# The order of VectorE's two maxima and its copy in each half of an attention quad

## The chip, the core and the metric

The kernel runs on one core of a Trainium2 chip. The time is the device time of one execution in microseconds, the median of several runs. TensorE (PE) does the matrix products and the transposes, VectorE (DVE) and ScalarE (ACT) read their results out of eight PSUM banks, GpSimd (POOL) does part of the elementwise work, SyncE (SP) issues DMAs. Each engine runs its own list of instructions strictly in the order in which the program writes them, and waits for the other engines through counters.

## What is computed

Four layers one after another on x of shape 4 x 512 x 512 in float32: a sparse-mask attention with grouped heads (layer 0), full attention with one key head and a gated MLP (layer 1), cosine attention and an MLP (layer 2), and a mixture of small per-chunk MLPs (layer 3). All are conditioned by a vector per batch. The change touches the softmax of the first three:

```python
# layer 0: 16 heads of 32, 4 key heads; keys limited by a block mask
scores = jnp.einsum('bhtd,bhsd->bhts', q, k_exp) / jnp.sqrt(jnp.asarray(HEAD_DIM, x.dtype))
scores = jnp.where(mask[None, None], jnp.asarray(-jnp.inf, x.dtype), scores)
attn = jax.nn.softmax(scores, axis=-1)
y = jnp.einsum('bhts,bhsd->bhtd', attn, v_exp)
# layer 1: 8 heads of 64, one key head, no mask
attn = jax.nn.softmax(scores, axis=-1)
# layer 2: 16 heads of 32
scores = jnp.einsum('bhqd,bhkd->bhqk', qn, kn) + attn_bias
p = jax.nn.softmax(scores, axis=-1)
```

## The kernel before

Attention is cut into units: one head and one tile of 128 queries. Layers 0 and 2 have 64 units per batch (16 heads x 4 query tiles), layer 1 has 32, and with 4 batches that makes 256, 128 and 256 units. In layer 0 a unit has 1 to 4 key tiles of 128, since later blocks are masked; in layers 1 and 2 always 4. Four neighbouring units form a quad, so the layers have 64, 32 and 64 quads.

A unit goes through these steps (class `Heads`):

- scores (PE, L655): q times k into one of four PSUM banks, the bank being the unit's number modulo 4 (banks 0 to 3).
- max (DVE): in layers 0 and 2 one instruction reads the scores' bank and the bias, writes their negated sum to the probability buffer `Pr` and leaves the row maximum in `nmax` (L735, with a short second record that reads the accumulator); it frees the scores' bank. In layer 1 a plain reduction (L739); there the exponential reads the bank and frees it.
- exp (ACT, L765): reads `Pr` (layer 1: the bank), writes `Pr`, sums the row.
- turn (PE, L663): transposes of `Pr`, one for each key tile, into bank 4 or 5 in turns.
- copy: the turned tile goes from PSUM to `PT`, on ACT for the quad's even units (L770), on DVE for the odd ones (L742).
- values (PE, L679): `PT` with v into bank 6, once for every 4 or 8 units; then out (ACT, L777), recip (DVE, L747), spread (PE, L689) and divide (DVE, L753) per block of 128 channels.

The function `weave` writes the one order from which all four engines take their lists. Its loop goes over quads. In round t it writes the scores of the four units of quad t+1, then the first half: turns 0 and 1 of quad t, the ACT copy of unit 0, max and exp of unit 0 of quad t+1, the DVE copy of unit 1, max and exp of unit 1 of quad t+1. Then come a point for other work, spreads, values of quad t-1, another point, and the second half with units 2 and 3 in the same pattern, and two more points. At the points `weave` inserts "side" work of other batches and layers: norms (L261 to L352), projections (L388), the rotary step (L426 to L451), output projections (L1281), for layer 2 also the query and key norms (L479 to L522), the splitting of MLP weights (L1064, L1068). After each attention stretch comes an MLP (L1024), after the last the experts of layer 3.

Which waits an instruction carries is worked out by the program: `claim` makes a PE step wait for the step that last read its bank, so the scores of unit n wait for the max (layer 1: the exp) of unit n-4, a turn waits for the copy of the turn two before. A wait that an earlier wait of the same engine already covers is left out.

Below, turn i, copy i, max i and exp i mean unit i of a quad, 0 to 3. In round t turns and copies belong to quad t, maxima and exponentials to quad t+1, and the scores that open round t+1 belong to quad t+2.

Of the kernel before, what the change touches and what calls it, by code (L numbers as in the profile page):

```python
# [832 lines left out]
def weave(tab, mains, sides, opening=(), closing=()):  # L833

    seq, quads = [], []
    for m, (h, b) in enumerate(mains):
        h.first[b] = len(tab.units)  # L840
        tab.units += [(h, b, u) for u in range(h.U)]
        for g in range(h.U // h.G):
            tab.group_number[(h.name, b, g)] = len(tab.groups)
            tab.groups.append((h, b, g))
        quads += [(m, h, b, q) for q in range(h.U // 4)]

    per = [sum(q[0] == m for q in quads) for m in range(len(mains))]
    at_point = {(0, i): list(ops) for i, ops in enumerate(opening)}
    at_point.update({(len(mains), i): list(ops) for i, ops in enumerate(closing)})
    for m, count in enumerate(per):  # L850
        points = 4 * count
        for i, ops in enumerate(sides[m]):
            at_point.setdefault((m, (2 * i + 1) * points // (2 * len(sides[m]))), []).extend(ops)
    seen = [0] * (len(mains) + 1)

    def point(m):
        seq.extend(at_point.get((m, seen[m]), []))
        seen[m] += 1

    def units(t):  # L860
        if 0 <= t < len(quads):
            _, h, b, q = quads[t]
            return [(h, b, 4 * q + i) for i in range(4)]
        return []

    def turn(t, i):
        for h, b, u in units(t)[i:i + 1]:
            seq.append((h, b, "pe", "turn", u))

    def copy(t, i):  # L870
        for h, b, u in units(t)[i:i + 1]:
            seq.append((h, b, "dve" if i % 2 else "act", "copy", u))

    def soft(t, i):
        for h, b, u in units(t)[i:i + 1]:
            seq.extend([(h, b, "dve", "max", u), (h, b, "act", "exp", u)])

    spreads = []
    for t in range(-1, len(quads) + 2):
        m = quads[t + 1][0] if t + 1 < len(quads) else len(mains)  # L880
        for h, b, u in units(t + 1):
            seq.append((h, b, "pe", "scores", u))
        turn(t, 0)
        turn(t, 1)
        copy(t, 0)
        soft(t + 1, 0)
        copy(t, 1)
        soft(t + 1, 1)
        point(m)
        for h, b, c in spreads:  # L890
            seq.extend([(h, b, "pe", "spread", c), (h, b, "dve", "divide", c)])
        spreads = []
        for h, b, u in units(t - 1)[3:]:
            if (u + 1) % h.G == 0:
                g = h.group(u)
                seq.append((h, b, "pe", "values", g))
                if g % 2:
                    seq.extend([(h, b, "act", "out", g // 2), (h, b, "dve", "recip", g // 2)])
                    spreads.append((h, b, g // 2))
        point(m)  # L900
        turn(t, 2)
        turn(t, 3)
        copy(t, 2)
        soft(t + 1, 2)
        copy(t, 3)
        soft(t + 1, 3)
        point(m)
        point(m)
    assert not spreads and seen[len(mains)] >= len(closing)
    return seq  # L910
# [194 lines left out]
def conditioned_stack(nc, a, out):  # L1105
    ctx = ExitStack()
    with ctx:
# [409 lines left out]
        def ahead(stage):  # L1517
# [11 lines left out]
        sides01.append(beats((norm1b, 0)) + [[]] * 4 + among(beats((post1, 2)), beats((pair1, 0)) + mlp1.split(0)) +  # L1529
                       beats((norm1b, 1), (pair1, 1), (norm1b, 2)) + [[]])  # L1530
        attention01 = weave(tab, [(heads0, b) for b in range(B)] + [(heads1, b) for b in range(B)], sides01,
                            closing=[[], first[0], [], first[1], first[2], first[3]])
        qk = beats((qk2, 0))
# [7 lines left out]
        sides2.append(beats((norm2b, 0)) + among(beats((post2, 2)), beats((pair2, 0)) + mlp2.split(0)) +  # L1541
                      beats((norm2b, 1)) + [[]])
        attention2 = weave(tab, [(heads2, b) for b in range(B)], sides2, opening=qk[7:],
                           closing=[[], first[0], [], first[1]])
        hidden2 = fold(parts, (0, 2, beats((pair2, 1))), (0, 4, beats((post2, 3))), (2, 3, mlp2.split(1)),
# [245 lines left out]
```

How the kernel before makes its waits and increments, by code:

```python
def start_wait(k, e, at, *names, but={}):  # L38
    for name in names:
        n = at[name] - but.get(name, 0)
        if n > 0:
            e.wait_ge(k.done[name], n)
# [19 lines left out]
    def dve(s, k, e, b, kind, index, after):  # L64
        if kind == "negate":
            for due in after(s.name, b, "sin", 0):
                e.wait_ge(*due)
            e.tensor_scalar(k.table[:, 2, :], k.table[:, 1, :], -1.0, None, ALU.mult).then_inc(k.done["dve"], 1)
            return
        steps = [0]
        def inc(ins):
            steps[0] += 1
            ins.then_inc(k.s_angle, 1)
            e.wait_ge(k.s_angle, steps[0])
        e.wait_ge(k.l_pos, 16 * (B + 1))
        ang, kk, r = (k.work[:, i, :] for i in range(3))
        inc(e.tensor_copy(kk, k.pos))
        inc(e.tensor_scalar(ang, kk, k.freq[:, 0:1], None, ALU.mult))
# [12 lines left out]
    def act(s, k, e, b, kind, index, after):  # L93
        for due in after(s.name, b, "reduce", 0):
            e.wait_ge(*due)
        k.act_set = "sin"
        src, out = (k.work[:, 4, :], k.table[:, 1, :]) if kind == "sin" else (k.work[:, 5, :], k.table[:, 0, :])
        e.activation(out, src, ACT.Sin).then_inc(k.done["act"], 1)
# [22 lines left out]
    def pe(s, k, e, b, kind, j, after):  # L121
        bank = s.tab.claim(e, s, b, kind, j, after)
        if kind == "block":
            if j == 0:
                e.wait_ge(*s.first_loaded)
                e.wait_ge(*s.cond_loaded)
            if j == 4:
                for due in after(s.name, b, "silu", 0):
```

## Time and profile before

| | us |
|---|---|
| median of 3 runs (2635.02 to 2640.76) | 2637.15 |
| the profiled execution, its own time | 2634.65 |
| its span, first to last instruction | 2632.9 |
| PE busy (share 94%) | 2475.2 |
| DVE busy (share 46%) | 1203.0 |
| ACT busy (share 42%) | 1104.3 |

In the profile's time axis the attention of layer 0 lies between about 85 and 505 us, that of layer 1 between 505 and 900, that of layer 2 between 1500 and 2140. The rest is MLPs, the experts, and the start. PE's busy time is modelled: a matmul that is held back while another is in flight can count as busy. So the waits are read from the chain of work that ended last, and from the idle times of PE's weight loads (PEld), rather than from PE's busy share.

### The profile page before, as it was taken

How to read it: one execution, taken by the hardware profiler on the slowest of the kernel's cores; microseconds unless marked ns; L12 is line 12 of the kernel's file. 1: busy time of each engine (PE TensorE's matmuls, PEld its weight loads, DVE VectorE, ACT ScalarE, POOL GpSimd, SP SyncE). 2: the span in 40 equal slices, each digit the busy share in tenths (PEclk: the TensorE clock that was granted, in tenths of full speed). 3: DMA queues.
4: the chain of work that ended last, by engine and by line, in shares of the span. 5: the costliest groups of instructions: out<-in, count | busy, mean ns of one | idle time of the engine just before them, and what ended most of it. 6: DMA issues, size and time to landing. Idle time of an engine off the chain costs nothing.

```text
span 2632.9 us, 32014 instructions
## 1 busy us (share of the span) xinstructions
PE 2475.2 (94%) x13000; PEld 1522.5 (58%) x13000; DVE 1203.0 (46%) x2466; ACT 1104.3 (42%) x2407; POOL 266.2 (10%) x222
## 2 busy tenths in 40 slices
PE   6889999999999899999999989999999898999998
PEld 2444455455454577888877544444444467888733
DVE  2464454543535554344433244637366654444323
ACT  2465555533444421111113255647456653222374
POOL 2331120220211100000001010101001010000021
PEclk8899999999999999999999979999998899999999
DMA  9100000000000000100001000000000010000001
GB/s 309 55 16 16 1 16 25 9 1 8 9 0 25 25 24 17 32 24 25 24 7 64 16 1 1 1 1 1 1 1 33 17 49 17 32 17 1 1 16 48
DMA packets 45235, 64.95 MB, mean 25 GB/s; under 512 B 8368, under 2 KB 21952, under 8 KB 45088
## 3 DMA queue, kind: packets, MB, share of 16 engines
q1 hardware_dynamic: 44112, 60.38, 7.1%
q0 software_dynamic: 976, 2.51, 0.3%
q8 instruction: 103, 1.69, 0.3%
q14 instruction: 44, 0.36, 0.0%
HBM read 52.66 MB, written 4.19 MB: 22 GB/s over the span
## 4 chain that ended last, share of the span: by engine, by line
PE 85%; DVE 9%; ACT 4%; POOL 1%; issue 1%; DMA 0%; SPq 0%; DVEq 0%; POOLq 0%; ACTq 0%
PE banks L1024 33%; PE banks L388 21%; PE banks L663 9%; PE banks L655 8%; PE banks L679 5%; DVE sb_Pr L735 2%; DVE sb_PT L742 2%; PE banks L689 2%; PE banks L486 1%; PE banks L261 1%; PE banks L561 1%; PE banks L426 1%; PE banks L569 1%; DVE sb_hN L352 1%; ACT sb_Pr L765 1%; ACT sb_PT L770 1%
## 5 line engine op out<-in xcount | busy, mean ns | idle before, releaser
L1024 PE MATMUL banks<-sb_HH,sb_Ws 128*128 128x512 f32 x1536 | 492.9, 394 | 12.8 <-DVE sb_HL L941 7.3
L765 ACT ACTIVATE sb_Pr<-sb_Pr,sb_nmax 128x512 f32<-128x512 f32 (+3 forms) x512 | 325.8, 637 | 117.4 <-DVE sb_nmax L735 115.5
L663 PEld LDWEIGHTS banks<-sb_ident,sb_Pr 128*128 128x128 f32 x2176 | 250.2, 146 | 201.1 <-issue 91.9
L655 PE MATMUL banks<-sb_R 32*128 32x512 f32 (+4 forms) x1280 | 311.8, 596 | 45.9 <-DVE sb_nmax L735 27.5
L742 DVE COPY sb_PT<-banks 128x512 f32<-128x512 f32 (+3 forms) x320 | 195.0, 609 | 328.6 <-PE banks L663 326.1
L663 PE MATMUL banks<-sb_ident,sb_Pr 128*128 128x128 f32 x2176 | 324.9, 290 | 19.4 <-ACT sb_PT L770 9.8
L1024 PEld LDWEIGHTS banks<-sb_HH,sb_Ws 128*128 128x128 f32 x1536 | 290.5, 189 | 78.1 <-issue 17.7
L735 DVE CUSTOM_DVE_ANT_0 sb_Pr<-banks,sb_bias 128x512 f32<-128x512 f32 (+3 forms) x512 | 290.6, 580 | 94.7 <-PE banks L655 94.0
L1024 PE MATMUL banks<-sb_hidH,sb_Ws 128*128 128x512 f32 x1024 | 332.2, 394 | 0.0
L770 ACT ACTIVATE sb_PT<-banks 128x512 f32<-128x512 f32 (+3 forms) x320 | 169.1, 529 | 342.0 <-PE banks L663 341.6
L1024 PE MATMUL banks<-sb_HL,sb_Ws 128*128 128x512 f32 x768 | 300.6, 391 | 0.0
L388 PE MATMUL banks<-sb_hN,sb_W 128*128 128x512 f32 x576 | 268.4, 610 | 7.8 <-ACT sb_hN L321 4.8
L655 PEld LDWEIGHTS banks<-sb_R 32*128 32x128 f32 (+1 forms) x1280 | 106.7, 190 | 202.6 <-DVE sb_nmax L735 84.3
L1024 PEld LDWEIGHTS banks<-sb_hidH,sb_Ws 128*128 128x128 f32 x1024 | 192.2, 188 | 43.5 <-issue 3.5
L1024 PE MATMUL banks<-sb_hidL,sb_Ws 128*128 128x512 f32 x512 | 199.3, 389 | 0.0
L388 PE MATMUL banks<-sb_A,sb_W 128*128 128x512 f32 x384 | 178.4, 608 | 2.4 <-DVE sb_x L1281 2.4
L388 PEld LDWEIGHTS banks<-sb_hN,sb_W 128*128 128x128 f32 x576 | 107.3, 195 | 125.0 <-issue 107.7
L679 PE MATMUL banks<-sb_PT,sb_V 128*32 128x256 f32 (+2 forms) x2304 | 169.8, 381 | 0.0
L1076 DVE TENSOR_TENSOR sb_tiles<-sb_tiles,banks 128x512 f32<-128x512 f32 x64 | 44.0, 688 | 272.4 <-PE banks L1024 272.4
L1051 ACT ACTIVATE sb_hidH<-sb_tiles 128x512 fp32r<-128x512 f32 x128 | 81.0, 632 | 200.4 <-DVE sb_tiles L1076 198.4
L1024 PEld LDWEIGHTS banks<-sb_HL,sb_Ws 128*128 128x128 f32 x768 | 145.3, 189 | 31.8 <-issue 2.2
L1046 ACT ACTIVATE sb_tiles<-banks,sb_cols 128x512 f32<-128x512 f32 x64 | 44.1, 689 | 237.6 <-PE banks L1024 237.6
(128 smaller groups left out, 2524.0 us busy)
## 6 DMA issues: line engine op xcount, KB each, us to landing
sb_staged<-in_L_cond_Wfc SPq DMA_DIRECT2D x16, 512.0 KB, 4.3
sb_wada<-in_L_cond_Wada SPq DMA_DIRECT2D x6, 1024.0 KB, 5.7
sb_x<-in_x SPq DMA_DIRECT2D x4, 1024.0 KB, 9.7
sb_staged<-in_L_cond_Wg SPq DMA_DIRECT2D x8, 512.0 KB, 3.4
sb_staged<-in_L_cond_Wu SPq DMA_DIRECT2D x8, 512.0 KB, 4.5
sb_staged<-in_L_cond_Wd SPq DMA_DIRECT2D x8, 512.0 KB, 3.6
out_x<-sb_x SPq DMA_DIRECT2D x4, 1024.0 KB, 4.5
sb_R<-sb_R SPq DMA_DIRECT2D x60, 64.0 KB, 2.0
```

The lines of the kernel that those rows point to most:

```text
L388: mm = e.matmul(bank[:, columns], lhsT, rhs, start=start, stop=stop)
L655: mm = e.matmul(bank[:, 0:s.width(u)], s.q(b, c)[rows, i * P:(i + 1) * P], s.k(b, c)[rows, 0:s.width(u)], start=True, stop=True)
L663: mm = e.transpose(bank[:, j * P:(j + 1) * P], k.Pr[:, n % 6, j * P:(j + 1) * P], k.ident[:])
L679: mm = e.matmul(bank[rows, 2 * P * ip + skip:2 * P * (ip + 1)], s.v(b, j, s.vhead(c, hl)), s.PT[:, n % 2, hl, j, skip:2 * P], start=j == 0 ...
L689: mm = e.matmul(bank[hl * s.dv:(hl + 1) * s.dv, i * P:(i + 1) * P], k.rsum[:, b % 2, o:o + 1].to_broadcast([P, s.dv]), k.ident[:], start=T ...
L735: ins = e.tensor_tensor_reduce(k.Pr[:, n % 6, 0:s.width(u)], S, k.bias[:, s.units[u][2], 0:s.width(u)], -1.0, 3.0e38, ALU.add, ALU.min, s. ...
L742: ins = e.tensor_copy(*s.turned(k, b, u))
L765: ins = e.activation(prob, prob if s.biased else k.bank(n % 4)[:, 0:s.width(u)], ACT.Exp, bias=s.stat(k, k.nmax, b, u), scale=-1.0 if s.bi ...
L770: ins = e.activation(*s.turned(k, b, u), ACT.Copy)
L1024: mm = e.matmul(bank, lhsT, rhs, start=i == 0, stop=i == len(mats) - 1)
L1046: ins = e.activation(k.tile(t), bank, ACT.Gelu_apprx_tanh, bias=s.hbias[:, f:f + 1], scale=1.0)
L1051: ins = e.activation(k.hidH[:, st % 2, t, :], k.tile(t), ACT.Copy)
```

## The change

In each half of a round the DVE list gets max 1 in front of copy 1, and max 3 in front of copy 3. Nothing is added, removed or resized, in all 160 quads and both halves.

```diff
         turn(t, 1)
         copy(t, 0)
         soft(t + 1, 0)
+        soft(t + 1, 1)
         copy(t, 1)
-        soft(t + 1, 1)
         point(m)
...
         copy(t, 2)
         soft(t + 1, 2)
+        soft(t + 1, 3)
         copy(t, 3)
-        soft(t + 1, 3)
         point(m)
         point(m)
```

`soft` writes a DVE max and an ACT exp, and copies 1 and 3 are DVE's, so only DVE's list changes its order. ACT's list stays as it is. PE's list keeps its order too, but carries other waits.

DVE in layer 2, the round and a half ahead of the side norm L337 (the ISA rows of L735 are a max and the read of its accumulator, the COPY is copy 1 or copy 3), before:

```order
L735 ISA sb_Pr,sb_nmax<-banks,sb_bias 128x512
L735 ISA sb_nmax 128x1
L742 COPY sb_PT<-banks 128x4x128 [waits pe_done]
L735 ISA sb_Pr,sb_nmax<-banks,sb_bias 128x512
L735 ISA sb_nmax 128x1
L735 ISA sb_Pr,sb_nmax<-banks,sb_bias 128x512 [waits pe_done]
L735 ISA sb_nmax 128x1
L742 COPY sb_PT<-banks 128x4x128 [waits pe_done]
L735 ISA sb_Pr,sb_nmax<-banks,sb_bias 128x512
L735 ISA sb_nmax 128x1
```

and with the change:

```order
L735 ISA sb_Pr,sb_nmax<-banks,sb_bias 128x512
L735 ISA sb_nmax 128x1
L735 ISA sb_Pr,sb_nmax<-banks,sb_bias 128x512
L735 ISA sb_nmax 128x1
L742 COPY sb_PT<-banks 128x4x128 [waits pe_done]
L735 ISA sb_Pr,sb_nmax<-banks,sb_bias 128x512 [waits pe_done]
L735 ISA sb_nmax 128x1
L735 ISA sb_Pr,sb_nmax<-banks,sb_bias 128x512 [waits pe_done]
L735 ISA sb_nmax 128x1
L742 COPY sb_PT<-banks 128x4x128 [waits pe_done]
```

Before, the rows read max 0, copy 1, max 1, max 2, copy 3, max 3. Now they read max 0, max 1, copy 1, max 2, max 3, copy 3; each copy has gone behind the maximum that followed it.

PE at the same place: the end of turn 3, the four scores (L655), then turns 0 and 1 (L663, four transposes each), before:

```order
L663 MATMUL banks<-sb_ident,sb_Pr 128x128 x3
L655 MATMUL banks<-sb_R 128x512
L655 MATMUL banks<-sb_R 128x512 [waits dve_done] x3
L663 MATMUL banks<-sb_ident,sb_Pr 128x128 [waits act_done]
L663 MATMUL banks<-sb_ident,sb_Pr 128x128 x7
L261 MATMUL banks<-sb_t,sb_ones 128x512 [waits pool_done]
```

and with the change:

```order
L663 MATMUL banks<-sb_ident,sb_Pr 128x128 x3
L655 MATMUL banks<-sb_R 128x512 x2
L655 MATMUL banks<-sb_R 128x512 [waits dve_done] x2
L663 MATMUL banks<-sb_ident,sb_Pr 128x128 [waits act_done]
L663 MATMUL banks<-sb_ident,sb_Pr 128x128 x3
L663 MATMUL banks<-sb_ident,sb_Pr 128x128 [waits dve_done]
L663 MATMUL banks<-sb_ident,sb_Pr 128x128 x3
L261 MATMUL banks<-sb_t,sb_ones 128x512 [waits pool_done]
```

Before, one score of the four carried no wait and three waited for DVE, and turn 1 had no wait of its own, since the wait for max 3 covered copy 3. Now two scores wait for DVE, and turn 1 carries its own wait for copy 3, which stands behind max 3.

## Rows read from the trace of the kernel before

**Rows 1.** The page's chain that ended last, shares of the span by engine
```profile
PE 85%; DVE 9%; ACT 4%; POOL 1%; issue 1%; DMA 0%; SPq 0%; DVEq 0%; POOLq 0%; ACTq 0%
```

**Rows 2.** Attention stretches: busy us of PE, PEld, DVE, ACT, POOL; granted clock; DMA
```profile
85.00:505.00 420.00, 380.95 (x2648) 203.19 (x2648) 216.29 (x721) 241.65 (x698) 82.73 (x66) 0.95 0.05 13
505.00:900.00 395.00, 371.71 (x2015) 199.58 (x2016) 189.31 (x313) 176.36 (x410) 59.96 (x47) 0.97 0.04 13
1500.00:2140.00 640.00, 597.20 (x3680) 301.70 (x3673) 339.68 (x792) 359.77 (x799) 41.52 (x33) 0.94 0.02 7
```

**Rows 3.** Groups of instructions by form: count | busy us, mean ns | idle before
```profile
L742 DVE COPY sb_PT<-banks 128x512 f32<-128x512 f32 x224 | 154.4, 689 | 259.2 <-PE banks L663 258.6
L735 DVE CUSTOM_DVE_ANT_0 sb_Pr<-banks,sb_bias 128x512 f32<-128x512 f32 x320 | 214.3, 681 | 71.5 <-PE banks L655 71.5
L770 ACT ACTIVATE sb_PT<-banks 128x512 f32<-128x512 f32 x224 | 132.7, 592 | 273.7 <-PE banks L663 273.7
```

**Rows 4.** Chain, layer 2, first and last bare wait: start us, us, what
```profile
1544.82 0.69 DVE sb_PT L742
1545.51 0.59 DVE sb_Pr L735
...
2096.62 0.60 DVE sb_Pr L735
```

**Rows 5.** Chain, layer 0, first and last bare wait
```profile
119.59 0.69 DVE sb_PT L742
120.29 0.20 DVE sb_Pr L735
...
468.20 0.59 DVE sb_Pr L735
```

**Rows 6.** Chain through one whole round of layer 2
```profile
1667.92 0.69 DVE sb_PT L742
1668.61 0.59 DVE sb_Pr L735
...
1669.21 0.60 DVE sb_Pr L735
...
1669.83 0.60 DVE sb_PT L742
1670.43 0.59 DVE sb_Pr L735
...
1671.09 1.12 PE banks L655 x2
1672.21 1.04 PE banks L663 x8
```

**Rows 7.** DVE's timeline, same round: start us, us, instruction [idle before <-releaser]
```profile
1670.95 0.69 DVE L735 CUSTOM_DVE_ANT_0 sb_Pr<-banks,sb_bias 128x512 f32<-128x512 f32 x1
...
1673.27 0.69 DVE L742 COPY sb_PT<-banks 128x512 f32<-128x512 f32 x1 [1.63 <-PE banks L663]
```

**Rows 8.** PE's weight loads, same round
```profile
1671.09 0.29 PEld L655 LDWEIGHTS banks<-sb_R 32*128 32x128 f32 x2 [0.92 <-DVE sb_nmax L735]
```

**Rows 9.** Chain, layer 1: copy 3 and, behind max 3, exp 3
```profile
657.75 0.60 DVE sb_PT L742
...
658.98 0.79 ACT sb_Pr L765 x2
```

**Rows 10.** Who waited for whom: us in total, times, longest us
```profile
ACT sb_Pr L765 <- DVE sb_nmax L735: 115.5, 210, 10.7
PEld banks L655 <- DVE sb_nmax L735: 84.3, 106, 3.2
PE banks L663 <- DVE sb_PT L742: 1.1, 2, 0.5
```

**Rows 11.** Chain, layer 2, after a long DVE stretch: PE at half clock
```profile
2063.29 3.28 PE banks L655 x4
2066.57 1.90 PE banks L663 x8
```

## Prediction

> **What bounds the kernel now.** The first thing to read is the chain of work that ended last: 85% of it is PE, 9% DVE, 4% ACT [rows 1]. PE is the bound, and an order on DVE can only pay where PE stands still for DVE. So the second view is the chain cut into the three attention stretches, the only places that the change touches. They take 420, 395 and 640 us, in which DVE is busy for about half the time and ACT for 45 to 58% [rows 2]: neither is full on average, so what counts is the order of their work around a PE wait. I went along the chain and took every stretch in which it leaves PE. In the three layers these sum to 89, 84 and 132 us, and the piece that comes back again and again is copy, then max, then a score on PE.
>
> The mechanism is in one round of layer 2 without side work [rows 6]. Turn 1 ends, and the chain goes through copy 1 (0.69), max 1 (0.59), max 2 (0.60), copy 3 (0.60), max 3 (0.59), then the one score that waited for max 3 (1.12), then turns 0 and 1 (1.04), and again. From 1667.92 to 1673.25 that is 5.33 us. Yet DVE stands idle for 1.63 us at its end, waiting for turn 1 [rows 7], although max 1 needs only a score that PE has finished before the turns. PE's weight load for the last score waited 0.92 us [rows 8]. Over the kernel such loads waited 84.3 us for L735, 106 times, while turns waited for a DVE copy for 1.1 us in all [rows 10]. The maxima are late and the copies are early; the change takes from the copies and gives to the maxima.
>
> **The change part by part.** No instruction is added or removed; a 512 wide copy keeps its 689 ns, a 512 wide max its 681 [rows 3]. Back to back each costs the chain 0.60. The waits fall in four kinds.
>
> (a) Bare waits: turn 3 ends, copy 3, max 3, score. There are 8 in layer 2, of 0.69 + 0.59 = 1.28 us [rows 4], and 12 in layer 0, eight of 0.69 + 0.20 = 0.89 (narrow max) and four of 0.56 + 0.59 = 1.15 (narrower copy) [rows 5]. Together 8 x 1.28 + 8 x 0.89 + 4 x 1.15 = 21.9 us. With max 3 in front, DVE takes it while it would stand idle for turn 3, and the whole wait can go. In eight of the twenty that idle time is shorter than the max, so some 3 us stay: 19.
>
> (b) Longer waits that end in max, copy 3, max 3, score, as in the round above. Max 3 comes one copy earlier: 14 in layer 2 x 0.60, 8 in layer 0 x about 0.47 (three tiles wide) = 12 us. In layer 1 exp 3 stands between max and score [rows 9], and exp 3 also stands behind exp 2 on ACT. ACT's waits for L735 average 115.5 / 210 = 0.55 [rows 10], the most that an earlier max can give; I take 0.3 for six of them: 2 us.
>
> (c) Waits that open with copy 1 and max 1 and go on over DVE: max 1 leaves the path, since it now runs in the idle time in front of copy 1 (1.63 here, [rows 7]). 16 of them x 0.60 = 10 us.
>
> (d) Waits that go copy 1, max 1, exp 1, and on to side work on ACT: ACT gets exp 1 earlier by what it waited, about 0.45, eight times: 4 us.
>
> Gross: 19 + 12 + 2 + 10 + 4 = 47 us.
>
> What is late next? In the side-free round the new chain is copy 1 (0.69), max 2, max 3 (0.60 each), score (1.12), turns (1.04), with issue 4.1 us. ACT needs four exponentials of 0.79 [rows 9] and two copies of 0.59 [rows 3], 4.34 us, so it allows 0.99 of the 1.23 us that the chain would give: a fifth is lost. I apply that fifth everywhere, for the side steps on DVE (0.6 to 2.4 us) that sit between the halves too. 47 x 0.8 = 38 us.
>
> The costs. Each copy 1 or 3 comes later by at most one max, 0.60, and nothing at all where DVE stood idle. Behind copy 3 is turn 1 of the next quad. PE does a score and turn 0 first, 1.12 + half of 1.04 after max 3 ends, and the copy is done 0.69 after it: covered by about 0.9. Behind copy 1 is turn 3, with turn 2 in front of it, and values, spread or side work in most rounds; if nothing of that stands there the cover is half of 1.04, and max 1 must be done when turn 1 ends. Counted from max 3's end, copy 3, max 0 and max 1 take 1.8 us and score and turns 2.2: a cover of 0.4, which one side step of 0.69 eats. The new waits that PE carries for these copies have no row; a wait that is already met shows no gap where the old order had one, so I take zero, with 160 x 0.02 (an "issue" piece of the chain) = 3 us as the upper end, and nothing speaks for a gain from them.
>
> The maxima can't be held up by data that come later than the copy's own: PE's list has all four scores in front of turns 0 and 1. The Trainium skill, page "PSUM — Partial Sum Buffer", section "Engine vs sequencer instructions", says that VectorE's queue is strictly first in, first out, which speaks against putting a max in front of a copy that is ready. By that rule alone every copy that DVE could have taken at once would come 0.60 later; the rows have turns waiting for copies 1.1 us in total, so the sum gives it nothing.
>
> **The clock.** After a DVE stretch that held PE for nearly 5 us, the scores took 3.28 and two turns 1.90 instead of 1.12 and 1.04 [rows 11]: PE ran at the lower of its two levels, 1.2 GHz, and lost 3.0 us. The three stretches have mean clocks of 0.95, 0.97 and 0.94 [rows 2], so several such spells lie in each. Shorter waits may end some of them, and a shifted pattern may make others; I put +-10 us in the range and nothing in the sum.
>
> **Sum.** 2634.65 (the profiled execution) - 38 = 2596.6. The median of the runs before lies 2.5 above that execution, so 2599.
>
> **The rivals.**
> 1. Hidden anyway: the waits go, but another step is nearly as late everywhere (ACT's exponentials, turn 3 behind copy 1), so that only about a third of the 47 is kept. For: in layer 1 ACT stands in the path [rows 9]. Against: ACT is idle for nearly half of the stretches. 2637 - 15 = 2622. A stronger form leaves nothing at all: about 2635.
> 2. Slower: copy 1, now behind max 1, becomes what turn 3 waits for. It decides from the point where DVE still has side steps to do when the scores come, so that max 1 is not done at the end of turn 1. The price is 0.60 for each of 160 first-half copies, 96 us at most; if 100 were late, +60 - 38 = +22, 2659. For: half of the rounds have no values between turns 1 and 3. Against: DVE stood idle before two thirds of its copies, and turns never waited for them.
> 3. A bonus from the clock: five spells at half clock vanish, 5 x 3.0 = 15 us more, 2584. The Trainium skill, page "TensorE: Matmul & The Clock Gate", Part 1, has the clock fall after PE has been idle and rise after sustained work; by that rule shorter waits could give this bonus, and the trace agrees that the slow matmuls follow the longest wait. Against: the longest waits are made of side work (L1068, L352, L337) and shrink by only 0.6 to 1.2.
> 4. The edit doesn't do what it says: excluded by the order of the changed list, where every max 1 and max 3 stands in front of the copy.
>
> **How the numbers follow.** Forecast 0.58; rival 1 at 2622 0.13, in its form without effect 0.11; rival 2 0.08; rival 3 0.10. The measurement can tell about 0.2% (5.3 us) from no change. Faster: 0.58 + 0.13 + 0.10 = 0.81; same 0.11; slower 0.08. The range goes from rival 3 with the clock term's 10 us below, 2574, to just beyond rival 1, 2632; it leaves out rival 2, about half of no change, and a little at the low end.
>
> **What would show it.** Right, step by step: the chain's copy share falls, and in a side-free round of layer 2 copy 1 follows two maxima and is followed by two more, with the round at 4.3 to 4.5 us instead of 5.33; PE's weight loads wait far less than 84.3 us for L735; DVE's idle time in front of L742 falls by about one max where it was long; ACT's waits for nmax fall. In the windows, layers 0 and 2 give about 16 and 18 us, layer 1 about 4. Wrong: the chain shows copy 1 followed by turn 3 many times, PE's waits for the DVE copy rise from 1.1 us to tens; or the rounds are as short as forecast and the time returns in waits for side work (L388, L261) further on.

## The result and the profile after

The changed kernel takes 2549.8 us (median of 4 runs, 2549.0 to 2552.9) against 2636.1 of the kernel before (4 runs, 2626.4 to 2640.8). The ratio is 0.9683, with a 95% interval of 0.9656 to 0.971: about 84 us or 3.2% faster. The direction of the forecast was right; its size was not. It had 38 us, and its range ended at 2574. A few executions of the kernels below ran far slower than the rest of their kernel (one of 5289 us, and the profiled one of "copy 1 only" with 2812 us, of which therefore only the times are used) and stand outside of the ratios.

The page of the changed kernel, the chain's shares by engine, answers to [rows 1]:

```profile
PE 87%; ACT 6%; DVE 5%; POOL 1%; issue 1%; DMA 0%; SPq 0%; DVEq 0%; POOLq 0%; ACTq 0%
```

DVE's share of the chain falls from 9% of 2633 us to 5% of 2547 (239 us to 122), ACT's rises from 4 to 6% (100 us to 158). The stretches that correspond to those of [rows 2] (same columns; they start a few us earlier, since the start was shorter too):

```profile
80.00:475.00 395.00, 362.16 (x2663) 194.66 (x2667) 214.96 (x725) 232.64 (x702) 83.40 (x68) 0.96 0.05 14
475.00:855.00 380.00, 358.28 (x2002) 195.05 (x1996) 189.82 (x310) 169.74 (x407) 59.94 (x47) 0.99 0.05 13
1454.00:2055.00 601.00, 562.95 (x3674) 292.65 (x3669) 337.41 (x791) 349.13 (x799) 41.61 (x33) 0.95 0.02 6
```

By these round ends they are 25, 15 and 39 us shorter, and 28, 13 and 38 when the same PE records mark the ends; 16, 4 and 18 were forecast. DVE's busy time hardly moves (216, 189, 340 before): the instructions are the same, they stand elsewhere. The granted clock is 0.01 to 0.02 higher in each. Who waited for whom (us in total, times, longest), which answers to [rows 10]:

```profile
PEld banks L655 <- DVE sb_nmax L735: 33.8, 61, 3.2
ACT sb_Pr L765 <- DVE sb_nmax L735: 47.1, 43, 10.8
DVE sb_PT L742 <- PE banks L663: 199.2, 135, 4.9
PE banks L663 <- DVE sb_PT L742: 3.0, 2, 1.5
```

The score's weight loads waited 84.3 us for L735 before and 33.8 now, ACT's exponentials 115.5 and 47.1. DVE's idle time in front of its copies was 326.1 us in 199 places and is 199.2 in 135. Turns wait 3.0 us for DVE's copies instead of 1.1: the copies, though later, are still in time. So the mechanism is the forecast one. It shows in the side-free round of layer 2 of [rows 6], now by DVE's timeline (start us, us, instruction, idle before it):

```profile
1614.46 0.68 DVE L735 CUSTOM_DVE_ANT_0 sb_Pr<-banks,sb_bias 128x512 f32<-128x512 f32 x1
...
1615.07 0.68 DVE L735 CUSTOM_DVE_ANT_0 sb_Pr<-banks,sb_bias 128x512 f32<-128x512 f32 x1
...
1615.68 0.69 DVE L742 COPY sb_PT<-banks 128x512 f32<-128x512 f32 x1
1616.34 0.69 DVE L735 CUSTOM_DVE_ANT_0 sb_Pr<-banks,sb_bias 128x512 f32<-128x512 f32 x1
...
1616.96 0.69 DVE L735 CUSTOM_DVE_ANT_0 sb_Pr<-banks,sb_bias 128x512 f32<-128x512 f32 x1
...
1618.00 0.69 DVE L742 COPY sb_PT<-banks 128x512 f32<-128x512 f32 x1 [0.34 <-PE banks L663]
```

Maxima 2 and 3, copy 3, maxima 0 and 1, copy 1. DVE now stands idle for 0.34 us in front of copy 1, not 1.63 [rows 7]. The chain of the same round (start, us, what) has no DVE piece left; an ACT copy of 0.61 us is in it, and the three pieces from 1614.16 on are turns, scores, turns:

```profile
1613.41 0.61 ACT sb_PT L770
1614.02 0.14 issue
1614.16 1.10 PE banks L663 x8
1615.25 1.68 PE banks L655 x8
1616.93 1.02 PE banks L663 x8
```

From the start of one turn 0 to that of the next, this round took 5.35 us before (5.33 as the chain cuts it) and takes 4.15 now. It shrank by 1.2, two DVE instructions, and ended below the 4.3 to 4.5 of the forecast. One wait for a max is still there, under the scores' 1.68 us:

```profile
1615.81 0.29 PEld L655 LDWEIGHTS banks<-sb_R 32*128 32x128 f32 x2 [0.32 <-DVE sb_nmax L735]
```

### Where the 86 us are

The chain cuts the time differently in the two kernels, so I compared them by PE's own records. PE's list has the same 13,000 instructions in both, and by their starts in the same order but for six pairs of neighbours, so the time from the start of one record to the start of the next can be subtracted, record by record. The total is 85.7 us between the two profiled executions. A score group below is the stretch from the first to the last of the eight score records (L655) that open a round; there are 160.

| where, worked out from start times of PE's records | forecast, us | measured, us |
|---|---|---|
| score groups, 69 rounds in which the chain of before left PE there | 34 (43 less a fifth) | 54.4 |
| score groups, 91 rounds in which that chain stayed on PE | 0 | 15.9 |
| everything else behind the first score | 3 | 11.1 |
| in front of the first score, where the change does nothing | 0 | 4.3 |
| sum | 38 | 85.7 |

By layer the score groups gave 29.4, 8.2 and 32.5. By the kinds of the forecast: the 20 bare waits gave 22.2 (forecast 19), the longer waits that end in max, copy 3 and max 3, of which the chain has 26 and not 22, gave 19.4 (12), the six of layer 1 gave 4.7 (2), all others 8.1.

The second line of the table could have been seen before. This is the chain of the kernel before in a round which it books on PE alone:

```profile
1642.01 1.82 PE banks L655 x7
1643.82 1.02 PE banks L663 x8
```

PE's weight loads in the same stretch:

```profile
1642.70 0.29 PEld L655 LDWEIGHTS banks<-sb_R 32*128 32x128 f32 x2 [0.67 <-DVE sb_nmax L735]
```

and the chain where nothing holds the scores:

```profile
1697.86 1.07 PE banks L655 x8
```

Eight records take 1.07 us when they are free and seven took 1.82 here, because the last pair waited 0.67 for a max. Of the 91 rounds that the chain books on PE, 21 have such waits of a weight load for L735, 13.3 us in all, and these 21 gave about 13 of the 15.9 us. The four scores use 32 rows of PE each and run beside one another (their eight records take 1.07 us, two of them alone 1.12 [rows 6]), so while an earlier one is in flight the wait of a later one lies under a busy PE, and the chain has no DVE piece for it.

### The profile page after: what moved, and what is told of

Same layout as the page of the kernel before. It is cut to its first block, busy times and chain, and to the rows that moved or that the text cites. A ratio compares the mean times of both kernels' runs of the same rounds, so it can differ in the third digit from the quotient of the medians.

```text
span 2547.1 us, 32014 instructions
## 1 busy us (share of the span) xinstructions
PE 2401.9 (94%) x13000; PEld 1497.4 (59%) x13000; DVE 1200.0 (47%) x2466; ACT 1077.9 (42%) x2407; POOL 265.9 (10%) x222
## 4 chain that ended last, share of the span: by engine, by line
PE 87%; ACT 6%; DVE 5%; POOL 1%; issue 1%; DMA 0%; SPq 0%; DVEq 0%; POOLq 0%; ACTq 0%
PE banks L1024 34%; PE banks L388 22%; PE banks L663 9%; PE banks L655 8%; PE banks L679 5%; PE banks L689 2%; ACT sb_Pr L765 2%; PE banks L486 2%; PE banks L261 1%; PE banks L426 1%; ACT sb_PT L770 1%; PE banks L561 1%; PE banks L569 1%; DVE sb_hN L352 1%; DVE sb_Pr L735 1%
## 5 line engine op out<-in xcount | busy, mean ns | idle before, releaser
L663 PEld LDWEIGHTS banks<-sb_ident,sb_Pr 128*128 128x128 f32 x2176 | 244.6, 144 | 201.0 <-issue 87.7
L765 ACT ACTIVATE sb_Pr<-sb_Pr,sb_nmax 128x512 f32<-128x512 f32 (+3 forms) x512 | 322.3, 633 | 48.0 <-DVE sb_nmax L735 47.1
L663 PE MATMUL banks<-sb_ident,sb_Pr 128*128 128x128 f32 x2176 | 318.6, 286 | 22.0 <-ACT sb_PT L770 11.3
L735 DVE CUSTOM_DVE_ANT_0 sb_Pr<-banks,sb_bias 128x512 f32<-128x512 f32 (+3 forms) x512 | 279.2, 582 | 103.2 <-PE banks L655 102.5
L742 DVE COPY sb_PT<-banks 128x512 f32<-128x512 f32 (+3 forms) x320 | 194.5, 608 | 199.6 <-PE banks L663 199.2
L655 PE MATMUL banks<-sb_R 32*128 32x512 f32 (+4 forms) x1280 | 256.3, 593 | 29.6 <-DVE sb_nmax L735 13.4
L655 PEld LDWEIGHTS banks<-sb_R 32*128 32x128 f32 (+1 forms) x1280 | 93.5, 189 | 145.8 <-issue 84.4
```

What stands on the lines that cost most here:

```text
L655: mm = e.matmul(bank[:, 0:s.width(u)], s.q(b, c)[rows, i * P:(i + 1) * P], s.k(b, c)[rows, 0:s.width(u)], start=True, stop=True)
L663: mm = e.transpose(bank[:, j * P:(j + 1) * P], k.Pr[:, n % 6, j * P:(j + 1) * P], k.ident[:])
L735: ins = e.tensor_tensor_reduce(k.Pr[:, n % 6, 0:s.width(u)], S, k.bias[:, s.units[u][2], 0:s.width(u)], -1.0, 3.0e38, ALU.add, ALU.min, s. ...
L742: ins = e.tensor_copy(*s.turned(k, b, u))
L765: ins = e.activation(prob, prob if s.biased else k.bank(n % 4)[:, 0:s.width(u)], ACT.Exp, bias=s.stat(k, k.nmax, b, u), scale=-1.0 if s.bi ...
```

## The experiments

Each is timed beside the kernel before. A difference between two changed kernels is the difference of their ratios times 2636 us; by the intervals it is uncertain by 8 to 10 us. The edits are shown against the kernel before, unless another is named.

### Each half alone, and layer 1 alone

Only max 3 in front of copy 3 (the first half of the round as before):

```diff
         soft(t + 1, 2)
+        soft(t + 1, 3)
         copy(t, 3)
-        soft(t + 1, 3)
```

> Only the second half is changed: max 3 in front of copy 3; the first half stays copy 1, max 1. Theory A (what counts is how early max 3 frees the scores' bank, since the last of the four scores waits for it): this half alone gives most of the 86 us, as the kinds (a) and (b) of the prediction, 33 of its 47 us, belong to it: 55 to 70 us faster, about 2570 to 2580. Theory B (the gain comes from DVE getting rid of work while it stands idle for the turns, wherever that is, and each half does its half): about 40 us faster, near 2595. Theory C (the halves need each other, since max 2 and 3 can only be early when max 1 is out of the way): under 30 us.

2577.7 us, ratio 0.9781 (0.9759 to 0.9803): 58 us faster than before, as theory A has it.

Only max 1 in front of copy 1 (the second half as before):

```diff
         soft(t + 1, 0)
+        soft(t + 1, 1)
         copy(t, 1)
-        soft(t + 1, 1)
```

> Only the first half is changed: max 1 in front of copy 1; the second half stays copy 3, max 3. Theory A: it takes max 1 from the long chains alone (kinds (c) and (d), 14 of 47 us): 15 to 30 us faster, about 2610 to 2620. Theory B: about 40 us faster. Theory C: near nothing alone. If the sum of this and of the second half alone is near 86 us, the halves act apart.

2618.5 us, ratio 0.994 (0.9923 to 0.9957): 16 us. The two sum to 74 of the 84 us, so the halves act nearly apart. By the forecast's terms the second half was (a) and (b), 26 us after the fifth, and the first half (c) and (d), 11 us. The second one is the one that was too small. In the score groups alone, max 3 in front gave 63.0 us and max 1 in front 6.8, which sum to 69.8 of the 70.3 of both.

The new order only where the maxima belong to layer 1, in both halves:

```diff
+        early = any(not h.biased for h, b, u in units(t + 1))
+        if early:
+            soft(t + 1, 1)
         copy(t, 1)
-        soft(t + 1, 1)
+        if not early:
+            soft(t + 1, 1)
...
+        early = any(not h.biased for h, b, u in units(t + 1))
+        if early:
+            soft(t + 1, 3)
         copy(t, 3)
-        soft(t + 1, 3)
+        if not early:
+            soft(t + 1, 3)
```

> Both halves are changed, but only where the quad of the maxima is of layer 1, where ScalarE's exponential frees the scores' bank. Compared instruction by instruction, the two traces give layer 1 13 us of the 86. If the layers act apart, this is 10 to 16 us faster (about 2623). If it is under 5 us, layer 1's share in the full change came from elsewhere, such as PE's clock in that run.

2614.8 us, ratio 0.9934 (0.9909 to 0.9958): 17 us (11 to 24), where the score groups gave 7.1. At least a third of it, and by the middle value more than half, lies elsewhere.

### Are the copies now late, and how much room do they have?

All four maxima in front of copy 1, ACT's order untouched:

```diff
-    def soft(t, i):
+    def most(t, i):
         for h, b, u in units(t)[i:i + 1]:
-            seq.extend([(h, b, "dve", "max", u), (h, b, "act", "exp", u)])
+            seq.append((h, b, "dve", "max", u))
+
+    def exps(t, i):
+        for h, b, u in units(t)[i:i + 1]:
+            seq.append((h, b, "act", "exp", u))
...
         copy(t, 0)
-        soft(t + 1, 0)
+        most(t + 1, 0)
+        exps(t + 1, 0)
+        most(t + 1, 1)
+        exps(t + 1, 1)
+        most(t + 1, 2)
+        most(t + 1, 3)
         copy(t, 1)
-        soft(t + 1, 1)
...
         copy(t, 2)
-        soft(t + 1, 2)
+        exps(t + 1, 2)
+        exps(t + 1, 3)
         copy(t, 3)
-        soft(t + 1, 3)
```

> The full change taken further: VectorE takes all four maxima in front of copy 1, then copy 1, and copy 3 alone in the second half; ScalarE's order stays. Copy 1 now comes up to two maxima (1.2 us) later than in the changed kernel, max 2 and 3 come earlier. Theory A with slack behind the copies gone (the slower rival of the prediction, one step further): turn 3 waits for copy 1, and the kernel is 10 to 40 us slower than the changed kernel, 2560 to 2590. Against it, if copies still have cover and the maxima were still late: up to 15 us faster than the changed kernel, about 2535 to 2550.

2542.4 us, ratio 0.9648 (0.9633 to 0.9662): 9 us faster than the change, where I had expected it to be slower. Here turns do wait for copies (who waited for whom, as above):

```profile
PE banks L663 <- DVE sb_PT L742: 30.1, 29, 2.9
PE banks L663 <- ACT sb_PT L770: 34.2, 25, 5.7
```

This is the forecast's second rival at work, 3.0 us grown to 30.1. It is outweighed: of the scores' waits for a max 0.6 us is left at the weight loads and 0.3 at the matmuls, and the score groups are 131.5 us shorter than before instead of 70.3. So the change itself leaves room that a max can still take.

The next one keeps the four maxima early, but lets copy 1 go in front of maxima 2 and 3:

```diff
         most(t + 1, 1)
         exps(t + 1, 1)
-        most(t + 1, 2)
-        most(t + 1, 3)
         copy(t, 1)
+        most(t + 1, 2)
+        most(t + 1, 3)
```

> A cross between the changed kernel and the one with four maxima first: VectorE takes max 0, max 1, copy 1, max 2, max 3 in the first half and copy 3 alone in the second, so that max 2 and 3 stand in front of the side steps between the halves but copy 1 isn't pushed behind them. With four maxima first the waits of the transposes for VectorE's copy rose to 30 us while the waits for maxima vanished. Theory A: this keeps the second and avoids most of the first, 5 to 25 us faster than four maxima first, 2518 to 2538. If the copy's lateness is not what the first one paid, it is within 4 us of it.

2532.3 us, ratio 0.9619 (0.9594 to 0.9644): the fastest of all, 17 us faster than the change and 4% faster than before. Its waits:

```profile
PE banks L663 <- ACT sb_PT L770: 36.4, 25, 5.7
PE banks L663 <- DVE sb_PT L742: 5.2, 3, 1.8
PE banks L655 <- DVE sb_nmax L735: 0.3, 1, 0.3
PEld banks L655 <- DVE sb_nmax L735: 3.4, 10, 0.6
```

Both kinds of wait for DVE are nearly gone: 3.4 us in front of the score's weight loads, against 33.8 with the change and 84.3 before, and 5.2 for copies. What is left is ACT: the turns' waits for its copy rose from 11.3 us with the change to 36.4.

### What a slower copy costs in either order

A reduction of the same bank into a spare column, ahead of each of DVE's 320 copies. It takes about 0.6 us at 512 columns, 168 us over all 320 from start to start, and computes nothing that is used:

```diff
+            o = (s.first[b] + u) // 2 % 80
+            e.tensor_reduce(k.spare[:, o:o + 1], s.tab.at[(s.name, b, "turn", u)][:, 0:s.width(u)], AX_X, ALU.max,
+                            negate=True)
             ins = e.tensor_copy(*s.turned(k, b, u))
```

The kernel before, unchanged, once more in this group:

> The kernel before once more, with its own profile, to see what of the 86 us between the two profiled executions is chance. The gap between the halves and layers summed from traces and the times says that the first 4 us (before the first score) are chance, and that PE's time at half clock (83.6 us of lost clock before, 58.0 after) may be partly chance. Expected: same time, a ratio within 0.998 to 1.002, the score groups of the 160 rounds within 2 us of the first profile, and lost clock within 8 us of 83.6. If lost clock comes out near 58 here too, the clock has no part in the gain.

2636.1 us, ratio 1.0003 (0.9984 to 1.0021). Its profiled execution had a span of 2624.2 us, the first one 2632.9. So these two executions of one kernel differ by about 9 us by chance. Of these, 4 lie in front of the first score.

The kernel before with the slower copies:

> The kernel before, with each of VectorE's 320 copies of turned tiles made slower: a reduction of the same bank into a spare column runs in front of the copy, 0.6 us at 512 columns, less for narrow tiles. Theory A (copies 1 and 3 stand on the path to the scores, since max 1 and max 3 come behind them): every round in which the copy already was exposed gives the whole 0.6, and more rounds become exposed; 60 to 110 us slower, about 2700 to 2745. If the copies had slack as large as 0.6 in front of the maxima: under 25 us.

2746.5 us, ratio 1.0421 (1.0399 to 1.0443): 111 us more.

The changed kernel with the slower copies:

> The changed kernel with the same slower copies. Theory A: the copies have nothing urgent behind them any more but the next two maxima, and turns wait for them only after a score and a turn; the same 0.6 us now costs little, 5 to 30 us over the changed kernel, 2555 to 2580. Rival (VectorE is full enough in the busy rounds that any added work counts, so the order only moved the wait): 60 us or more, as in the kernel before.

2591.5 us, ratio 0.9836 (0.9816 to 0.9856): 40 us more than the change without them. The same work on DVE costs 111 us in the old order and 40 in the new one. That is the mechanism shown directly: before, what DVE does in a copy stands in front of a score; after, most of it doesn't. The waits say the same. In the kernel before, repeated, and then with slow copies:

```profile
PEld banks L655 <- DVE sb_nmax L735: 84.5, 106, 3.2
PE banks L655 <- DVE sb_nmax L735: 27.6, 38, 2.5
```

```profile
PEld banks L655 <- DVE sb_nmax L735: 124.5, 109, 3.2
PE banks L655 <- DVE sb_nmax L735: 58.8, 67, 2.8
```

In the changed kernel with slow copies (the copy's line is L745 there), the score's weight loads wait as long as without them, and the turns' waits for the copy are what grows, from 3.0:

```profile
PEld banks L655 <- DVE sb_nmax L735: 34.0, 57, 3.2
PE banks L663 <- DVE sb_PT L745: 16.6, 32, 2.3
```

But 40 us was also more than I had expected, so the copies have less cover than the forecast had given them. To see which one, the reduction stood ahead of one of the two alone, on the changed kernel.

Ahead of copy 1 only (`if u % 4 == 1:` in front of the reduction):

> The changed kernel with the added reduction (0.6 us at 512 columns) in front of copy 1 alone. With it in front of all 320 copies the changed kernel became 40 us slower. The prediction gave copy 1 a cover of 0.4 us at most and copy 3 one of 0.9. If that holds, nearly all of the 40 us is here: 28 to 38 us over the changed kernel, about 2580 to 2588. If the added time counts because VectorE is full, whichever copy it is, it is about 20 us: near 2570.

2573.1 us, ratio 0.9768 (0.9751 to 0.9784): 22 us more than the change.

Ahead of copy 3 only (`if u % 4 == 3:`):

> The same in front of copy 3 alone. With a cover of 0.9 us behind copy 3: 2 to 10 us over the changed kernel, about 2552 to 2560. If VectorE's load is what counts: about 20 us, near 2570, and this and the one for copy 1 add up to the 40.

2566.8 us, ratio 0.9744 (0.9726 to 0.9762): 16 us more. 22 + 16 = 38, nearly the 40 of both. I had expected nearly all of it from copy 1, and that falls. Either copy costs, copy 3 hardly less. That is what the other case of both expectations had, about 20 us each if DVE's load is what counts, whichever copy carries it. In the trace of the last one, turns wait 7.7 us for DVE's copy instead of 3.0, and time grew in the step from one turn record to the next, by 7.9 us, and in steps at half clock, by 3.6.

### Does the same order pay on ACT?

In both halves both maxima and exponentials in front of both copies, on ACT as well as on DVE:

```diff
-        copy(t, 0)
         soft(t + 1, 0)
-        copy(t, 1)
         soft(t + 1, 1)
+        copy(t, 0)
+        copy(t, 1)
...
-        copy(t, 2)
         soft(t + 1, 2)
-        copy(t, 3)
         soft(t + 1, 3)
+        copy(t, 2)
+        copy(t, 3)
```

> The changed kernel with the same swap on ScalarE: exp 0 and 1 in front of copy 0, exp 2 and 3 in front of copy 2. If the rule is 'the step that PE needs first goes first', this loses: an exponential in layers 0 and 2 is needed only by a turn one round later, a copy by the turn two further on, so copies 0 and 2 come up to 1.5 us later for nothing: 10 to 40 us slower than the changed kernel, 2560 to 2590, with most of it in layers 0 and 2, and less or a gain in layer 1, where the exponential frees the scores' bank. If instead 'fill the idle time in front of a copy' is the rule, ScalarE's idle time in front of L770 (346 us) would be filled as VectorE's was, and it is 5 to 20 us faster.

2641.1 us, ratio 1.0033 (1.0014 to 1.0052): the whole gain is gone, 92 us more than the change. For DVE the order is that of the change; only ACT's copies moved. What PE waits for now:

```profile
PE banks L663 <- ACT sb_PT L770: 60.6, 65, 5.6
PE banks L689 <- ACT sb_PT L770: 51.1, 39, 3.1
PEld banks L655 <- DVE sb_nmax L735: 26.8, 51, 3.2
```

and what ACT waits for in front of its exponentials:

```profile
ACT sb_Pr L765 <- DVE sb_nmax L735: 310.9, 143, 10.9
```

With the change the waits for ACT's copy were 11.3 and 12.9 us, and ACT's for the max 47.1. The scores' waits for the max stay as low as with the change. On ACT it is the copy that PE needs, since it frees the bank of the turn or spread two later, and here it must wait for two maxima and two exponentials. ACT now stands idle for a max with a copy behind it.

The fastest kernel, with exponentials 2 and 3 moved up behind their maxima:

```diff
         copy(t, 1)
         most(t + 1, 2)
+        exps(t + 1, 2)
         most(t + 1, 3)
+        exps(t + 1, 3)
...
         copy(t, 2)
-        exps(t + 1, 2)
-        exps(t + 1, 3)
         copy(t, 3)
```

> The order that was fastest so far (max 0, max 1, copy 1, max 2, max 3 in the first half) with exp 2 and exp 3 moved to the first half on ScalarE too, so that they aren't behind copy 2 and the side steps. In layer 1 an exponential frees the scores' bank, so there it can still give something; in layers 0 and 2 it has a round of slack. Expected within 6 us of that kernel, 2526 to 2538, with a gain of up to 6 us in layer 1; more than 10 us slower if side work on ScalarE (L321, L327, L299) was just in time.

2553.2 us, ratio 0.9695 (0.9677 to 0.9712): 20 us slower than with the exponentials left where they were, where I had expected a difference within 6. Again the ACT copy, now copy 2, came behind exponentials, and the turns' waits for ACT's copy went from 36.4 to 45.7 us; by PE's records, 17 of the 20 us lie in steps at half clock and 11 in the step from the scores to turn 0, with 7 given back inside the scores.

## Why the forecast's direction held and its size did not

**What held.** PE is the bound and DVE's order pays where PE waits for it. The max is late, the copy early, and the swap takes the max out of PE's wait; the slow-copy pair shows it (111 against 40 us). The second half is worth several times the first. A new wait of turns for copies stays near zero (3.0 us). Layer 1 gives least. The first rival, another step nearly as late everywhere, would have kept only a third of 47 us; more than the 47 came. The second rival, slower by late copies, did not happen; it appears only where all four maxima go first, at 30 us of waits, and even there the kernel is faster.

**The step that failed first: what was counted.** "I went along the chain and took every stretch in which it leaves PE." The chain does not leave PE when a score of 32 rows waits beside others that run. These rounds gave 15.9 us, and the forecast had none for them. PE's weight loads had shown such waits: of the 106 for L735 [rows 10], 25 lie in rounds that the chain books on PE, 13.3 of the 84.3 us.

**The terms.** The 20 bare waits gave 22.2 us and not 19: the 3 us that I let stay because DVE's idle time was shorter than the max did not stay. The longer ones were 26 and not 22, ten in layer 0 and 16 in layer 2, and gave 19.4 and not 12; in three rounds of layer 2 like the one shown the saving was 1.21 and not 0.60, since max 1 left the path too, which the forecast had under (c). Layer 1 gave 4.7 and not 2. With the other rounds the visible waits gave 54.4 against 43 gross.

**The fifth.** "ACT needs four exponentials of 0.79 and two copies of 0.59, 4.34 us." The round came out at 4.15, below that floor. The durations in a row run over the next instruction's start. On ACT in the changed kernel, same round:

```profile
1615.32 0.58 ACT L770 ACTIVATE sb_PT<-banks 128x512 f32<-128x512 f32 x1
1615.80 0.71 ACT L765 ACTIVATE sb_Pr<-sb_Pr,sb_nmax 128x512 f32<-128x512 f32 x1
...
1616.50 0.71 ACT L765 ACTIVATE sb_Pr<-sb_Pr,sb_nmax 128x512 f32<-128x512 f32 x1
```

From start to start an exponential with its accumulator read takes 0.70 and the copy 0.48, so ACT's floor is 4 x 0.70 + 2 x 0.48 = 3.8 us. For DVE I had taken the 0.60 from start to start, for ACT the whole durations. ACT's load was no floor, and since more than the gross sum was gained, no run shows the fifth, 9 us. Still ACT is what the chain goes to next: its pieces there grew by 58 us, the exponentials' from 22 to 41 and the copies' from 19 to 33, while DVE's fell by 116. So ACT came in through single steps that PE or DVE wait for, not through its load.

**The covers.** I gave copy 3 a cover of 0.9 us and copy 1 one of 0.4, and argued that a later copy costs nothing. For the move itself the result was right, since turns wait 3.0 us for DVE's copies. The sizes were not: with 0.9 us of cover everywhere, 0.6 more ahead of copy 3 would cost nothing, and it costs 16 us. That the cover is thin where side work sits on DVE is my reading; no run took the side work away.

**The clock.** "I put +-10 us in the range and nothing in the sum." Time lost by the granted clock (each stretch's time times one minus its clock) was 85.1 us in the first profile of before, 78.3 in the second, 58.6 after the change. Spells at the lower level, 1.2 GHz, went from 27 and 25 to 20. The saving in the score groups is not made of this: against the second profile of before it is 70 us, of which 64 in steps at full clock in both. Outside of the groups, steps that were at 1.2 GHz before and at 2.4 after, less those of the other direction, gave about 10 us. That is the third rival's bonus, smaller than its 15, and it came together with the forecast's case instead of in its place. The slow copies show it from the other side. The kernel before, repeated, and then with slow copies, in the stretch of layer 2 (columns as in [rows 2]; the second is longer):

```profile
1500.00:2140.00 640.00, 601.04 (x3703) 307.21 (x3700) 343.14 (x797) 361.05 (x802) 45.84 (x36) 0.95 0.03 9
```

```profile
1500.00:2250.00 750.00, 684.64 (x3846) 348.60 (x3845) 428.55 (x939) 371.77 (x816) 41.58 (x33) 0.90 0.03 8
```

The clock falls from 0.95 to 0.90, the spells go from 25 to 45, and the lost time from 78 to 137 us over the kernel. Of the 115 us between these two profiles, 47 lie in score steps at full clock and 58 in steps touched by half clock. So in this pair the waits in front of the scores cost about as much again in steps touched by half clock. It is no fixed price: the kernel with all four maxima first waits less for DVE at its scores than the change does and has 18 spells, but loses 66 us by the clock. The Trainium skill, page "TensorE: Matmul & The Clock Gate", Part 1, has the clock fall after PE idles; the traces agree, with 45 spells where PE waited more and 20 where it waited less.

**Chance.** The first profiled execution of before took 2634.65 us, in the middle of that kernel's runs, the second 2626.31, among its fastest; against it the change's profile is 77 us shorter and not 85.7. By the timed runs the change is worth 84, with an interval of 76 to 91.

**Adding up.** From 38 to 86: 9 for the fifth, 11 for the visible terms (54.4 against 43), 16 for the waits that the chain books on PE, 7 for the rest behind the first score, mostly the clock, and 4 in front of the first score, where only chance acts: with their decimals, 48.

**Open.** What the 10 us of the clock outside of the score groups hang on is not settled: no run changed the waits and held the spells in place. Nor is it settled how much of the first half's 16 us is its own. Its score groups gave 6.8, and the interval of the ratio alone is +-4.5 us.

## What to carry to other kernels

- On an engine that serves a bound one, put first what frees the bank that the bound engine needs next. That was the max on DVE and the copy on ACT: with both of a half's other steps in front of the copy, the time went down by 3.2% on the one and up by 3.5% on the other. Split a pair of steps (max and exp) if their engines need different orders, and look how far ahead it pays: two maxima moved one half further gave another 17 us.
- To price a wait, don't count only where the chain leaves the bound engine. Look at its weight loads' waits, and at how long a group of matmuls takes free and held (1.07 and 1.82 us here). Floors of other engines come from start to start, not from durations.
- Put the clock on the side of the sign that the waits have, with a wide margin: here shorter waits in front of PE came with some 10 us by a higher clock, and longer ones, by 0.6 us ahead of each DVE copy, with as much again as they cost at full clock.

## What the runs showed of the hardware

- Four scores of 32 rows each run side by side: eight records in 1.07 us at full clock, so one late score hides under the others in the chain, which books them as PE.
- 168 us more on DVE, spread ahead of 320 copies, cost 111 us in one order and 40 in the other (60 to 110 and 5 to 30 were expected), on an engine that is busy for 46% of the span. In the old order half of it lay in steps touched by half clock.
- Exponentials of 128 x 512, each with its accumulator read, follow one another at 0.70 us, though their rows show 0.71 and 0.19.
